# The last pass of a graph network kernel: a short block in the seventh place, in two transfers, and the last full block as two halves

## The reference, cut to what matters

```
def _layernorm(x, axis=-1, eps=1e-05):
    m = jnp.mean(x, axis=axis, keepdims=True)
    v = jnp.var(x, axis=axis, keepdims=True)
    return (x - m) / jnp.sqrt(v + eps)
...
    x = _layernorm(x + _L0_gnn_ref(x, edge_index, edge_attr_32, ...), axis=-1)
    x = _layernorm(x + _L1_gnn_ref(x, edge_attr_128, src, dst, ...), axis=-1)
    return x
```

## Time and profile before

| what | value |
|---|---|
| device time, median of 3 runs | 4809.48 us |
| the three runs | 4803.77, 4809.48, 4822.28 us |
| span of the profiled execution | 4813.1 us |
| its own time beside the span | none is given |
| busy: PE, DVE, ACT, POOL | 3972.5, 3729.6, 3089.0, 2981.9 us |
| DMA over the span | 1002.80 MB, 208 GB/s |
| first load of the last pass | 4508.06 us |

### The profile page before, as it was taken

How to read it: one execution, slowest core, us unless ns; L and a number is a source line. 1 busy time by engine, 2 the same in 40 slices (tenths; PEclk the granted TensorE clock), 3 DMA queues, 4 the chain that set the end, 5 groups by cost and what they waited for, 6 DMA issues and landing times. The chain is left out here.

```text
span 4813.1 us, 84225 instructions
## 1 busy us (share of the span) xinstructions
PE 3972.5 (83%) x23546; PEld 3291.7 (68%) x23546; DVE 3729.6 (77%) x11631; ACT 3089.0 (64%) x7157; POOL 2981.9 (62%) x2765
## 2 busy tenths in 40 slices
PE   5899999977777499999999799999999999999200
PEld 3466666655555399999999687777788778777200
DVE  6899999978888699898989476666666666666564
ACT  6866666645555266666666477776777767776575
POOL 1055556567777355555555377777777778777322
PEclk9999999988999699999999899999999999999655
DMA  4255554558666499999999577766767766766696
GB/s 105 51 171 169 168 171 167 169 148 212 199 201 202 151 360 364 349 365 353 365 359 362 175 152 154 153 149 153 152 150 153 154 152 149 153 150 152 218 394 261
DMA packets 717533, 1002.80 MB, mean 208 GB/s; under 512 B 186862, under 2 KB 591298, under 8 KB 704182
## 3 DMA queue, kind: packets, MB, share of 16 engines
q0 software_dynamic: 160768, 323.45, 30.3%
q10 hardware_dynamic: 245565, 375.01, 21.6%
q1 hardware_dynamic: 310861, 300.30, 19.8%
HBM read 567.01 MB, written 431.82 MB: 208 GB/s over the span
## 5 line engine op out<-in xcount | busy, mean ns | idle before, releaser
L1468 PE MATMUL bank<-w0r,n_x1T 128*128 128x406 f32 x4704 | 903.3, 351 | 41.1 <-ACT n_pa L1516 38.9
L1468 PEld LDWEIGHTS bank<-w0r,n_x1T 128*128 128x128 f32 x4704 | 868.0, 189 | 65.6 <-ACT n_pa L1516 63.4
L1612 POOL DMA_INDIRECT out_x<-u_sums,u_row x392 | 635.8, 1622 | 144.4 <-issue 117.1
L1664 PE MATMUL bank<-u_h,w1r 128*108 128x512 f32 (+1 forms) x2646 | 692.4, 407 | 0.0
L635 POOL DMA_INDIRECT DS<-payload,rank_int x392 | 378.2, 965 | 477.0 <-DVE rank_int L810 386.5
L1344 POOL DMA_INDIRECT n_cg<-CT,n_last x392 | 452.0, 1153 | 174.4 <-issue 95.2
L1664 PEld LDWEIGHTS bank<-u_h,w1r 128*108 128x108 f32 (+1 forms) x2646 | 444.5, 175 | 129.8
L1595 POOL DMA_INDIRECT u_pa<-PA,key_int x392 | 388.2, 990 | 167.2 <-issue 120.1
L891 POOL DMA_INDIRECT xg<-XP,ds x392 | 412.4, 1052 | 125.9 <-issue 121.3
L1664 PE MATMUL bank<-w2r,u_h 108*128 108x256 f32 x3528 | 479.2, 280 | 0.0
L427 PE MATMUL bank<-wst,xT 128*128 128x264 f32 x1568 | 421.3, 391 | 51.0 <-DVE xps L436 50.8
(11 more groups left out here) (319 smaller groups left out, 10080.4 us busy)
## 6 DMA issues: line engine op xcount, KB each, us to landing
PA<-n_pa ACTq DMA_DIRECT2D x98, 816.0 KB
PB<-n_pb ACTq DMA_DIRECT2D x98, 812.0 KB
XP<-xps ACTq DMA_DIRECT2D x98, 528.0 KB
CT<-ct ACTq DMA_DIRECT2D x98, 528.0 KB
n_xp<-XP SPq DMA_DIRECT2D x98, 528.0 KB
xin<-in_x SPq DMA_DIRECT2D x97, 512.0 KB
n_x<-in_x SPq DMA_DIRECT2D x97, 512.0 KB, 9.8
out_x<-n_x ACTq DMA_DIRECT2D x97, 512.0 KB, 5.0
```

The source lines that it names most:

```text
L1468: o = nc.tensor.matmul(acc, xT[s][p][:, k, e], w0r[q][:, 2 * half + k, :], start=(n == 0), stop=(n == len(terms) - 1))
L1612: pool.indirect_dma_start(out=out, out_offset=bass.IndirectOffsetOnAxis(ap=si[s][:, j:j + 1], axis=0), in_=yo[s][:, j, :], in_offset=None, ...
L1664: o = nc.tensor.matmul(acc, a[p], b[q], start=(start and n == 0), stop=(stop and n == 2))
```

## The change

Only the last pass changes. The 848 rows of the short block are taken from the seventh place (index 6) and not from the end, so every later block starts 848 rows on and not 1024. Its load and its store are two transfers each, of 96 and of 10 partitions, on the same queue and counted on the same semaphore; `moved(b)` gives the count that a wait needs. Of the full blocks, 47 stay whole and the last is two blocks of 128 partitions with 4 rows each. There are 50 blocks for 49. The waits and the order of the engines' lists are otherwise as before; lines of the last pass move by some nine.

```
--- before.py
+++ after.py
@@ -1946,42 +1946,51 @@
             nm = [alloc(ph, f"f_shift{s}", [P, ROWS]) for s in range(2)]
             half = alloc(ph, "f_half", [P, ROWS])
             y_ld, o_st = sems("f_loaded", SLOTS), sems("f_stored", SLOTS)
-            f_init, f_chain, f_var, f_pow, f_nm, f_xo = (sem("f_init"), sem("f_chain"), sem("f_var"),
-                                                                 sem("f_pow"), sem("f_nm"), sem("f_xo"))
+            f_chain, f_var, f_pow, f_nm, f_xo = sem("f_chain"), sem("f_var"), sem("f_pow"), sem("f_nm"), sem("f_xo")
             FULL, left = divmod(N, P * ROWS)
-            assert left % ROWS == 0
-            BLOCKS = FULL + (left > 0)
-
-            def block_rows(b):
-                if b < FULL:
-                    return P, out[b * P * ROWS:(b + 1) * P * ROWS, :].rearrange("(p t) w -> p t w", t=ROWS)
-                return left // ROWS, out[FULL * P * ROWS:N, :].rearrange("(p t) w -> p t w", t=ROWS)
+            assert left % ROWS == 0 and FULL > 2 * SLOTS
+            HALF, SHORT = ROWS // 2, left // ROWS
+            SIXTEENTHS = SHORT // 16 * 16
+            sizes = [(P, ROWS)] * (FULL - 1) + [(P, HALF)] * 2
+            sizes.insert(SLOTS, (SHORT, ROWS))
+            starts = [sum(p * t for p, t in sizes[:b]) for b in range(len(sizes) + 1)]
+            BLOCKS = len(sizes)
+            assert starts[-1] == N and 0 < SIXTEENTHS < SHORT
+
+            def parts(b):
+
+                return [(0, SIXTEENTHS), (SIXTEENTHS, SHORT)] if b == SLOTS else [(0, P)]
+
+            def moved(b):
+
+                return 16 * (b // SLOTS + 1) + 16 * (b % SLOTS == 0 and b >= SLOTS)
+
+            def block_rows(b, p0, p1):
+                t = sizes[b][1]
+                return out[starts[b] + p0 * t:starts[b] + p1 * t, :].rearrange("(p t) w -> p t w", t=t)
 
             with nc.Block(no_gpsimd_drain=True) as block:
                 @block.sync
                 def _(sp):
-                    if FULL < SLOTS:
-                        sp.wait_ge(f_init, 1)
                     for b in range(BLOCKS):
-                        k, use = b % SLOTS, b // SLOTS
-                        need(sp, o_st[k], 16 * use)
-                        n, rows_ = block_rows(b)
-                        sp.dma_start(y[k][0:n], rows_).then_inc(y_ld[k], 16)
+                        k = b % SLOTS
+                        if b >= SLOTS:
+                            sp.wait_ge(o_st[k], moved(b - SLOTS))
+                        for p0, p1 in parts(b):
+                            sp.dma_start(y[k][p0:p1, 0:sizes[b][1]], block_rows(b, p0, p1)).then_inc(y_ld[k], 16)
 
                 @block.vector
                 def _(dve):
-                    if FULL < SLOTS:
-                        nc.vector.memset(y[FULL][:], 0.0).then_inc(f_init, 1)
                     c = Count(dve, f_chain)
 
                     def stats(b):
                         k, s = b % SLOTS, b % 2
-                        dve.wait_ge(y_ld[k], 16 * (b // SLOTS + 1))
-                        for j in range(ROWS):
+                        dve.wait_ge(y_ld[k], moved(b))
+                        for j in range(sizes[b][1]):
                             o = nc.vector.bn_stats(st[s][:, j, :], y[k][:, j, :])
                         c.step(o)
                         dve.sem_inc(dturn, 1)
-                        for j in range(ROWS):
+                        for j in range(sizes[b][1]):
                             o = nc.vector.bn_aggr(mv[s][:, j, :], st[s][:, j, :])
                         c.step(o)
                         need(dve, f_pow, b if b > 1 else 0)
@@ -2014,16 +2023,15 @@
                     for b in range(BLOCKS):
                         k, s = b % SLOTS, b % 2
                         act.wait_ge(f_nm, b + 1)
-                        for j in range(ROWS):
+                        for j in range(sizes[b][1]):
                             o = nc.scalar.activation(y[k][:, j, :], y[k][:, j, :], ACT.Identity,
                                                      bias=nm[s][:, j:j + 1], scale=rs[s][:, j:j + 1])
                         o.then_inc(f_xo, 1)
                         act.wait_ge(f_xo, b + 1)
-                        n, rows_ = block_rows(b)
-                        act.dma_start(rows_, y[k][0:n]).then_inc(o_st[k], 16)
-                    for k in range(SLOTS):
-                        if BLOCKS > k:
-                            act.wait_ge(o_st[k], 16 * ((BLOCKS - 1 - k) // SLOTS + 1))
+                        for p0, p1 in parts(b):
+                            act.dma_start(block_rows(b, p0, p1), y[k][p0:p1, 0:sizes[b][1]]).then_inc(o_st[k], 16)
+                    for b in range(BLOCKS - SLOTS, BLOCKS):
+                        act.wait_ge(o_st[b % SLOTS], moved(b))
 
 # ---- launch: one core; inputs and outputs as the reference has them ----
 _INS = ['x', 'src', 'dst', 'edge_attr_128', 'edge_attr_32', 'L0_gnn_lin_W', 'L0_gnn_att_src', 'L0_gnn_att_dst',
```

## The result

| | median | runs |
|---|---|---|
| before | 4812.94 us | 4803.77 to 4822.28 (4) |
| changed | 4777.40 us | 4772.86 to 4780.32 (4) |

The ratio is 0.9933 with a 95% interval of 0.9912 to 0.9953: 35.5 us, or 0.7%, faster. Forecast were 4774.7 us and 34.8 us less, in a range of 4765 to 4787. The changed kernel was measured twice more, beside the experiments, with ratios of 0.9922 (0.9905 to 0.9940) and 0.9922 (0.9907 to 0.9938).

The account below looks back on a forecast made before the run. Transfers bound the stream, and two-engine transfers of the short block its end. With 4.45 us displacement and ACT's list setting the end, the span fell from 4813.1 to 4778.3; 34.8 off the median 4809.5 gave 4774.7 us, range 4765 to 4787.

Parts of the forecast that it names:

- What bounds the kernel: Last pass: transfers set the pace; at its end the 106-partition load and store run on two of sixteen engines, share 0.12.
- Most of it is placement: Of the 34.8 us saved, most was credited to moving the short block, some 1.5 us to splitting the last full block.
- The displacement of 4.45 us: Stream behind index 6: the short block delays all that follows by 4.45 us, the upper end; 2.2 if only its store counts.
- The extra pieces: Second issues and 10-partition transfers are covered, costing nothing; rival (0.09): not covered, up to 6.4 plus 2.2 us more, 4783.3.
- the gap behind block 6: Stream after the short block: a gap there was named as a sign that the forecast is wrong.
- the bound of 6.4 us: Short block's 10 partitions: if all on one engine, 3.2 us a way, 6.4 for load and store; taken as nothing.
- The slower rival: Short block in mid-stream: its 96-partition transfer too stays on two engines, costing 39.9 against 34.8 won, 4815 us; chance 0.02.
- The end: Last blocks: ACT sets the end, 16.5 us from its fourth-last block; last store 2.8, from the third pass's 512 KB store.
- The fixed 2.0 us: Last store: the skill's fixed part of every transfer, besides bytes at 436 GB/s; 3.2 us for the half, ending 0.4 later.
- The margin of ACT: Last block: its shift is ready at 4770.5 at the latest, before ACT comes at 4773.1, with 2.6 us to spare.
- Its 1.5 us for the split: End: with the last full block undivided, ACT would work 4771.6 to 4775.6 and end about 4779.8, some 1.5 us worse.
- The sum: Whole kernel: span from 4813.1 to 4778.3, 34.8 us saved, taken off the median of 4809.5 to give 4774.7.

Follow-up runs that it names:

- the parts at the end: Against the kernel before: short block still last, last full block whole, only its load and store in 96 and 10 partitions; 4771.02 against 4801.38 us, ratio 0.9939.
- the halves alone: Against the kernel before: last full block in two halves, short block still last and in one transfer; one time of 4793.2 us.
- 53 and 53: Against the kernel before: short block still last, moved in two transfers of 53 partitions each way; one time of 4836.87 us.
- the ten first: Against the kernel before: short block last, in transfers of 10 then 96 partitions, the 10's store on its own semaphore; one time of 4769.06 us.
- the shared end: Against the changed kernel: DVE normalizes half the rows of the last three blocks; 4757.25 us beside 4765.49, measured again 4770.61 beside 4768.10.

## Why the prediction was right, point by point

**What bounds the kernel.** Right. The stretches of 0.12 were two engines; the transfer of 106 partitions alone, moved to the seventh place, keeps its cost (0.9991), and split at the old place it loses it (0.9939). The sentence "Most of it is placement" is wrong as it stands: the place alone gained nothing that the rounds can tell from zero, and the split of the transfers alone gained as much as the change, within the intervals. The sum didn't notice, because it only counts the slow transfers as gone from the end.

**The displacement of 4.45 us.** This is the step most likely off: "the short block has 848 of 1024 KB, so it displaces all that follows by 0.828 x 5.37 = 4.45 us", with 4.45 called its upper end. Five profiles without the short block in the stream (before, the parts at the end, the halves alone, 53 and 53, the ten first) have a lead of 249.2, 248.7, 244.5, 246.7 and 248.2 us, 247.5 on average. Eight with it, in two transfers, have 256.8, 253.6, 256.7, 254.9, 250.6, 254.4, 250.6 and 253.9, or 253.9. The difference is 6.5 us, with a standard error of 1.2 from the scatter within the two groups. So 4.45 is probably too low but not excluded; that it was an upper end has no support. Bytes may be the wrong measure for it: at the end of the program 848 KB in 96 and 10 took 5.3 us, where 1024 KB in one transfer took 4.4. That the same holds inside the stream fits the 6.5, but wasn't tried by itself.

**The extra pieces.** DVE begins block 6 at 4533.2, 7.5 us after its first load's issue (4525.7), and waits 5.0 us for block 7, where before it waited 7.4. But it waits 1.6 for block 8 and 4.4 for block 9, where before had 1.2 and 1.1. That is the gap behind block 6 which the forecast had named as a sign of being wrong. By block 9 the stream is 6.3 us behind that of before at block 8 (50.4 and 44.1 us after the first load); in the two repeats it is 1.6 and 5.2. The ten partitions are on ten engines, so the bound of 6.4 us for all ten on one engine wasn't reached; the second issue on ACT is 0.4 us and covered. The last store landed after 2.6, not 5.0.

**The slower rival.** Its mechanism was tried with one transfer in the seventh place: a lead of 282.7 is 35.2 more than 247.5, and 30.7 more than the 4.45 of the forecast's displacement. The rival had 39.9 for this, by two waits and a new filling of the stream. The lower bound of the expectation, two engines that simply set the pace (29.5), is the nearer one.

**The end.** 16.7 for 16.5 us: four activations take 2.07 and not 2.02, and the span ends some 0.6 us after the last landing, where I had 0.3, while the landing itself takes 2.6 and not 2.8. The fixed 2.0 us of the Trainium skill, page "DMA: Bandwidth & Descriptors", section "Anatomy of one DMA", would have made the landing 3.2: the measurement stands nearer to the row of the third pass. The forecast said that the section gives this for every transfer; it gives it for those issued from GpSimd, and this store is issued from ACT. The margin of ACT was said to be 2.6 us; the last shift came 1.1 us ahead of need, since POOL's power for block 49 waits for ACT's work on block 47, a wait that the forecast had left out. Its 1.5 us for the split was a slip: its own list has ACT free for the undivided block at 4770.69, not at 4771.6, and counted from there it comes to 0.7, as measured.

**The sum.** The pass of the changed kernel averages 272.4 us in three profiles, 32.6 less than the one profile of before. The forecast's own sum was 34.8: 2.0 of the difference is the lead, which is 6.5 us longer than in before and not 4.45, and 0.1 the end. The rounds show 35.5, 36.3 and 36.4 us; with one profile of before and a lead that varies by 3 us, what makes up the rest between 32.6 and these stays open. That the rounds come within 2 us of the 34.8 is therefore in part luck.

**What in the change does the work.** Not the place: it costs 6.5 us in the stream for what is at the end a block of similar length, and the pass is 273.4 with the short block last and 272.2 with it seventh, one profile each, which is less than the 3 us by which the pass of one kernel varies. The split of the last block is worth 0.7 us. The 96 and 10 partitions do all the rest.

## What to carry to other kernels

Look for long stretches at a small, constant DMA share: 0.12 is two of sixteen engines, and here the cause was the number of partitions of one transfer. Split it so that each part has a divisor of 16 or near it, and check the split by the small packets counted at its end; a wrong split (53 and 53) cost about as much as the right one gained. Don't split a transfer of 128 partitions into parts as here (96 and 32, 64 and 64), and mend a slow transfer before thinking about where it should stand.

## What the runs showed of the hardware that was not expected

- 1024 KB to memory on 16 engines took 4.4, 5.5 or 6.9 us (issue to end of span) as 128, as 96 and 32, or as 64 and 64 partitions.
- One transfer on two engines in a full stream of six buffers thinned the stream for 90 us and made the lead 35 us longer (282.7 for 247.5), about the 34 us that those engines need for it both ways.
- The fixed part of a store is small: 512 KB landed in 2.6 and 1024 KB in 3.9 us, so by an estimate from these two 1.3 us are left at no bytes.
- From 4600 to 4740 us the stream of the changed kernel ran at 390 GB/s in all three profiles, and that of the kernel with the shared end at 394 and 409. Their ends repeated to within 0.1 us (16.7 and 13.6).
